# Interleaving the two matmul runs of a fused transformer block's main loop on TensorE

## What is computed

```python
nx = _layer_norm(x, ln_gamma, ln_beta)
scores = einsum('bth,bph->btp', nx @ Wq, prototype_bank @ Wk) * H ** (-0.5)
evidence = einsum('btp,bph->bth', softmax(scores), prototype_bank @ Wv)
combined = concatenate([nx, evidence, anchor], axis=-1)          # (8, 512, 768)
router_probs = softmax(combined @ router_W + router_b)
h = silu(einsum('btc,ecr->bter', combined, e_w1) + e_b1)         # 3 experts x 512
expert_out = einsum('bter,erh->bteh', h, e_w2) + e_b2
routed = sum(expert_out * router_probs[..., None], axis=-2)
g = sigmoid(silu(combined @ gate_w1 + gate_b1) @ gate_w2 + gate_b2)
out = x + g * (routed @ out_w + out_b)
```

## Time and profile before

| what | value |
|---|---|
| median of 3 runs | 465.12 us (464.63 to 465.8) |
| span of the profiled execution | 462.2 us |
| PE (TensorE matmul) busy | 451.3 us, 98% of the span |
| PEld (weight load) busy | 400.3 us, 87% |
| DVE, ACT, POOL busy | 263.2, 236.0, 143.4 us |

### The profile page before, as it was taken

The page is one execution under the profiler, slowest core; times in us unless marked ns, Lnnn a source line. Parts: engine busy times, 40 slices in busy tenths (PEclk is TensorE's granted clock), DMA queues, the critical chain, the costliest instruction groups (busy, mean ns, idle before and its releaser), DMA issues.

```text
span 462.2 us, 7383 instructions
## 1 busy us (share of the span) xinstructions
PE 451.3 (98%) x2771; PEld 400.3 (87%) x2771; DVE 263.2 (57%) x574; ACT 236.0 (51%) x361; POOL 143.4 (31%) x200
## 2 busy tenths in 40 slices
PE   4999999999999999999999999999999999999995
PEld 4588888898988899898988999898988998988895
DVE  3567366758566554648456554648456655425336
ACT  1337455675645456634755456544754555644341
POOL 4104701009505620293005520392006520282000
PEclk9999999999999999999999999999999999999998
DMA  8577406121221322222311322222310312221001
GB/s 239 194 214 265 138 2 139 22 45 25 88 60 36 68 93 46 47 48 68 92 23 24 68 92 48 45 48 70 91 37 10 70 46 48 45 47 47 0 1 45
DMA packets 24611, 32.78 MB, mean 71 GB/s; under 512 B 1864, under 2 KB 16000, under 8 KB 24576
## 3 DMA queue, kind: packets, MB, share of 16 engines
q1 hardware_dynamic: 24256, 31.76, 26.4%
q0 software_dynamic: 240, 0.53, 0.5%
q10 hardware_dynamic: 80, 0.02, 0.0%
HBM read 13.40 MB, written 4.19 MB: 38 GB/s over the span
## 4 chain that ended last, share of the span: by engine, by line
PE 96%; DMA 1%; DVE 1%; issue 0%; SPq 0%; ACT 0%
PE bank L418 37%; PE bank L674 34%; PE bank L650 11%; PE bank L516 2%; PE bank L446 2%; PE bank L429 2%; PE bank L559 2%; PE bank L483 1%; DMA work<-in_ctx_dram 1%; PE bank L528 1%; PE bank L448 1%; PE bank L587 1%; PE bank L469 1%; PE bank L504 1%; PE bank L540 1%; PE bank L459 1%
## 5 line engine op out<-in xcount | busy, mean ns | idle before, releaser
L418 PE MATMUL bank<-nx,w1n 128*128 128x512 f32 x672 | 175.7, 397 | 0.0
L1106 DVE TENSOR_TENSOR h<-hf,h 128x512 fp32r<-128x512 f32 x112 | 83.5, 745 | 160.2 <-ACT h L828 159.3
L674 PEld LDWEIGHTS bank<-w,h 128*128 128x128 f32 x1152 | 149.8, 190 | 8.2
L674 PE MATMUL bank<-w,h 128*128 128x256 f32 x1152 | 152.0, 282 | 0.0
L825 ACT ACTIVATE hf<-bank,zb 128x512 f32<-128x512 f32 x112 | 77.2, 689 | 144.1 <-PE bank L650 143.9
L418 PEld LDWEIGHTS bank<-nx,w1n 128*128 128x128 f32 x672 | 119.3, 188 | 19.8
L828 ACT ACTIVATE h<-bank,zb 128x512 fp32r<-128x512 f32 x112 | 76.2, 681 | 0.0
L650 PE MATMUL bank<-wT,vw 128*128 128x512 f32 x224 | 69.9, 393 | 0.0
L1140 POOL TENSOR_TENSOR rstd<-ve,minus_half 128x4 f32<-128x4 f32 x8 | 9.1, 1136 | 159.1 <-DVE ve L853 159.1
L650 PEld LDWEIGHTS bank<-wT,vw 128*128 128x128 f32 x224 | 41.9, 188 | 9.0
L1150 POOL TENSOR_SCALAR work<-b2o,ph 128x256 f32<-128x256 f32 x32 | 20.8, 649 | 78.3 <-DVE ph L933 76.0
(11 more groups left out here) (127 smaller groups left out, 407.0 us busy)
## 6 DMA issues: line engine op xcount, KB each, us to landing
vw<-vw_pair SPq DMA_DIRECT2D x48, 256.0 KB, 3.7
stage<-in_L_xcond_e_w_dram SPq DMA_DIRECT2D x9, 512.0 KB, 4.5
xbuf<-in_x_dram SPq DMA_DIRECT2D x8, 512.0 KB, 4.4
out_dram<-xbuf SPq DMA_DIRECT2D x16, 256.0 KB, 2.1
vw<-vw_pair SPq DMA_DIRECT2D x16, 130.0 KB, 2.6
w1v<-in_L_xcond_e_w_dram SPq DMA_DIRECT2D x3, 512.0 KB, 6.3
work<-in_ctx_dram SPq DMA_DIRECT2D x1, 512.0 KB, 6.0
stage<-in_L_xcond_gate_w_dram SPq DMA_DIRECT2D x2, 256.0 KB, 9.6
```

The costliest lines, as they stand in the source:

```text
L418: mm = pe.matmul(dst, lhs(a), rhs(c), start=first and i == 0, stop=last and i == n - 1)
L674: mm = pe.matmul(o, h[:, s % HRING, a, t * PART:(t + 1) * PART], rhs, start=c == 0 and i == 0 and t % 2 == 0, stop=c == COUNT[g] - 1 and i ...
L1106: dve.tensor_tensor(h[:, s % HRING, LO, :], hf[:, s % 2, :], h[:, s % HRING, HI, :].bitcast(F32), ALU.subtract).then_inc(s_hlo, 1)
```

## The change

TensorE's two runs of a slot are issued in turn: one 512-wide matmul of block s, one 256-wide matmul of block s - 2, eight times, and then the four 256-wide ones that are left. The helpers `first_layer_nx`, `first_layer_evidence` and `second_layer` become `first_layer(s, i)` and `second_layer(s, n)`, which issue one matmul each; each wait is at the matmul that it stood at before. Slots 0 and 1, which have no second layer, keep their order, and so do the last two turns, which have no first layer. No instruction is added or taken away, and no other engine's order changes.

```diff
-            def first_layer_nx(s):
+            NX_PASSES = KC * len(SPLIT_PASSES)
+            Z_PASSES = NX_PASSES + 2
+            W_PASSES = NT * len(SPLIT_PASSES)
+
+            def first_layer(s, i):
...
+                dst = bank[ZB[s % 3]][:, :]
+                if i < NX_PASSES:
+                    k, (a, c) = i // len(SPLIT_PASSES), SPLIT_PASSES[i % len(SPLIT_PASSES)]
+                    pe.matmul(dst, w1n[:, a, k, j * PART:(j + 1) * PART], nx[:, b % 2, c, k, :],
+                              start=i == 0, stop=False)
+                    return
...
+                part = i - NX_PASSES
+                mm = pe.matmul(dst, vw[:, part, RP + j * PART:RP + (j + 1) * PART],
+                               wT[:, b % 2, :], start=False, stop=part == LO)
+                if part == LO:
+                    mm.then_inc(s_z, 1)
...
+            def second_layer(s, n):
...
+                t, i = divmod(n, len(SPLIT_PASSES))
+                half = t // 2
+                u = 2 * (NG * b + g) + half
+                if n == 0:
+                    pe.wait_ge(s_hlo, s + 1)
...
+                if c == 0 and t % 2 == 0 and i == 0:
+                    take(AB[u % 3], (s_comb, u + 1))
...
             for s in range(SLOTS + LAG):
                 b, j = divmod(s, NB)
+                if s == 0:
+                    for i in range(NX_PASSES, Z_PASSES):
+                        first_layer(s, i)
                 if s < SLOTS:
-                    if s == 0:
-                        first_layer_evidence(s)
                     run_plan(steps, "pe", b, j, "pre")
-                    if s >= EARLY:
-                        first_layer_nx(s)
-                    if s > 0:
-                        first_layer_evidence(s)
+                if 0 < s < LAG:
+                    for i in range(NX_PASSES, Z_PASSES):
+                        first_layer(s, i)
                 if s >= LAG:
-                    second_layer(s - LAG)
+                    for i in range(W_PASSES):
+                        if i < Z_PASSES and s < SLOTS:
+                            first_layer(s, i)
+                        second_layer(s - LAG, i)
```

More of the change, by code:

```diff
@@ L657, in second_layer @@
                 c = j - FIRST[g]
[L658 to L665, removed]
-                    u = 2 * (NG * b + g) + half
-                    if c == 0:
-                        take(AB[u % 3], (s_comb, u + 1))
-                    for t in (2 * half, 2 * half + 1):
-                        o = bank[AB[u % 3]][:, (t % 2) * H:(t % 2 + 1) * H]
-                        for i, (a, w) in enumerate(SPLIT_PASSES):
-                            rhs = gw2[:, w, c, :] if g == 0 else w2[:, w, j - GB, :]
-                            mm = pe.matmul(o, h[:, s % HRING, a, t * PART:(t + 1) * PART], rhs,
-                                           start=c == 0 and i == 0 and t % 2 == 0,
-                                           stop=c == COUNT[g] - 1 and i == 2 and t % 2 == 1,
-                                           skip_group_check=True)
-                    if half == 0 and c == COUNT[g] - 1:
-                        mm.then_inc(s_acc, 1)
@@ new lines, in second_layer @@
+                if c == 0 and t % 2 == 0 and i == 0:
+                    take(AB[u % 3], (s_comb, u + 1))
+                a, w = SPLIT_PASSES[i]
+                rhs = gw2[:, w, c, :] if g == 0 else w2[:, w, j - GB, :]
+                last = t % 2 == 1 and i == len(SPLIT_PASSES) - 1
+                mm = pe.matmul(bank[AB[u % 3]][:, (t % 2) * H:(t % 2 + 1) * H],
+                               h[:, s % HRING, a, t * PART:(t + 1) * PART], rhs,
+                               start=c == 0 and i == 0 and t % 2 == 0, stop=c == COUNT[g] - 1 and last,
+                               skip_group_check=True)
@@ L681, in second_layer @@
+                if last and c == COUNT[g] - 1:
                     mm.then_inc(s_acc, 1)
-                else:
+                elif last and half == 1:
                     mm.then_inc(s_w2, 1)
-            first_layer_nx(0)
+            for i in range(NX_PASSES):
+                first_layer(0, i)
             b2_product()
             w_transpose(0)
-            first_layer_nx(1)
+            for i in range(NX_PASSES):
+                first_layer(1, i)
             logits(0)
```

22 lines of the change are left out of this document (20 added, 2 removed).

## The result

The changed kernel takes 472.5 us (median of four runs, 471.69 to 473.09), the kernel before 465.09 in the same comparison (464.63 to 465.8): 7.4 us more, a ratio of 1.0156 with a 95% interval from 1.0139 to 1.0172. The prediction was 470.5 us, slower, in a range of 463.0 to 475.5.

What follows compares the result with a forecast made beforehand. PE's matmuls were taken to bound the kernel. Waits and end +8.0 us, cheaper pairs -3.1, longer waits from a shorter PE path +0.5: +5.4 on 465.12 gives 470.5 us, range 463.0 to 475.5.

Steps and rivals of the forecast that it cites:

- PE sets the time, and a matmul costs its distance to the next start: Whole kernel: PE busy 451.3 of 462.2 us, so time is the sum of matmul costs plus waits the new order makes.
- A pair at 344 ns, -3.1 us: Interleaved slots: one 512-wide plus one 256-wide costs 344 ns instead of 348, over 770 new pairs; between -6.2 and +2.3 us.
- 1.06 us of slack used up at every boundary: Group boundaries: matmul 6 asks for `combine` of half 0 1.06 us earlier; fourteen of 31 boundaries wait, 5.9 us.
- the rule: Group boundaries: each wait of matmul 6 is 1.06 us plus 0.05 for the semaphore, less the boundary's slack before.
- The price of a wait, 0.05 us on top: Group boundaries: each of the fourteen waits costs about 0.05 us more for the semaphore.
- Slack above zero is free: Group boundaries: seventeen with slack of 1.17 us or more, above the 1.06 us shift, stay free of waits.
- Slot 2 and slot 12: First batch: matmul 0 waits for L1106 in slot 2, +0.65 us; `w_transpose` waits behind DVE in slot 12, +0.6 us.
- Nothing else waits in the loop: Main loop: matmul 0 in later slots asks 2.44 us earlier against a smallest slack of 2.6, so stays free.
- The end, +0.83: Block 111: DVE's last chain hangs on the last first-layer matmul, which comes seven 256-wide matmuls later, +0.83 us.
- Rival 1: Pairs: a matmul's extra cost goes when widths alternate, pair 330 ns, 461.2 us; decides from 335 ns; chance 0.16.
- Rival 2: Group boundaries: the ACT and DVE chain gets shorter, so the 5.9 us of waits don't come, 464.1 us; chance 0.12.
- Rival 3: Pairs: each switch of bank and moving tile costs 5 ns, 10 a pair, 479.8 us; chance 0.10.

Runs made afterwards that it cites:

- A2: Changed kernel with DVE's `combine` of half 0 moved ahead of L1106, PE's order untouched: 465.17 us, ratio 1.0004 to the kernel before.
- B4: Kernel before, not interleaved, plus a DVE instruction of about 1 us ahead of `combine` of half 0 at group boundaries: 472.06 us, ratio 1.0138.
- A4: Changed kernel, but the two runs kept apart in the 32 slots whose second layer is a group's first block: 466.58 us, ratio 1.0029.
- B1: Changed kernel with A2's DVE order and the two runs kept apart in the first batch and slot 111: 462.22 us against 465.41, ratio 0.9935.
- B2: B1 with two 512-wide and three 256-wide matmuls in turn, four times a slot, instead of one and one: 467.21 us, ratio 1.0036.
- C1: Changed kernel with matmul 6's wait for `combine` moved onto the 512-wide matmul before it: 477.58 us against 465.4, ratio 1.0266.
- B3: Kernel before, but the 256-wide matmuls in the middle blocks of each expert alternate between their two banks: 465.35 us, ratio 0.9998.
- A1: Changed kernel, but slot 111, the last with a first layer, keeps its two runs apart: 471.44 us, ratio 1.0144.

## Why the prediction was right, and where it was short

- **PE sets the time, and a matmul costs its distance to the next start.** Right; with it the account closes to 0.1 us. The granted clock isn't full in every slice, as the prediction has it: the last slice of the earlier trace rows reads 8. It falls behind PE's last matmul, so nothing hangs on it.
- **A pair at 344 ns, -3.1 us.** The mean came out there (-3.3 us over some 770 new pairs, 4.3 each), but not for the reason given. I took a value between the costs at a switch and those inside a run. In fact more than half of the pairs have the lower bound of 340, and in 25 of the slots the mean is 348 to 349, near the upper one. All eleven slots that begin with 512-wide products are of the dear kind, but so are fourteen others; what decides is open, and the value of 344 is luck as much as reasoning. The Trainium skill ("TensorE: Matmul & The Clock Gate", "Back-to-back issue gap") has a formula for the gap of an isolated warm matmul, by which a pair would be estimated at 109 + 216 = 325 ns; the cheapest pairs here have 340, so taking the rows was right.
- **1.06 us of slack used up at every boundary.** Right, and the heart of the case: fourteen waits were predicted and fourteen came, at the very boundaries named, 6.0 us against 6.4. A2 removed them by DVE's order alone, B4 made thirteen of them by delay alone. That the sum came out so near is partly luck. In slots 16 and 18 the rule gives 1.06 and 0.49 us and the trace 0.53 and 0.02: in slot 16 PE had already lost 0.5 on the same path, at the pair product below, and in slot 17 L1106 took 1.24 us before and 0.73 in the changed kernel, for a reason that no run shows. The other twelve came to 5.4 us where the rule gives 4.7 with the cheaper pairs. The chain through ACT and DVE wasn't "as long as before" there: at nine of them it was 0.04 to 0.10 us longer, 0.7 in all.
- **The price of a wait, 0.05 us on top.** This is the step that fell short. A wait ends 0.05 to 0.06 us behind its releaser, as assumed, but then costs the restart of 0.105 as well: 14 x 0.105 = 1.5 us. It could have been read from the kernel before. In the earlier trace rows the first boundary has a slack of 0.05, and there two 256-wide matmuls have a duration of 0.51, where at the second boundary, with more slack, three have 0.52: one matmul's cost, 0.11, was lost already. The 0.05 there was no slack but the semaphore's own time; matmul 6 waited. I used the row for the slack and didn't look at what the small slack cost.
- **Slack above zero is free.** Also wrong, for 0.6 us. Matmul 6 in slot 32 of the changed kernel, PE:

```profile
173.38 0.40 PE L654 MATMUL bank<-wT,vw 128*128 128x512 f32 x1
173.62 0.35 PE L680 MATMUL bank<-w,h 128*128 128x256 f32 x1
173.81 0.40 PE L654 MATMUL bank<-wT,vw 128*128 128x512 f32 x1
```

It isn't late (0.24 behind its neighbour) and still takes 0.19 instead of 0.115. Its load could run ahead by a part only. The traces give the size: where half 0 was read 0.05 us ahead of matmul 6, matmul 6 took 0.105 us more; with 0.075 it took 0.09 more, with 0.09 it took 0.07, with 0.115 (B4) 0.04, and with 0.16 or more (A4, A2) nothing. Read time and extra cost add up to 0.16 us throughout, the semaphore's 0.055 and a load's 0.105. So to be free a matmul needs what it waits for 0.16 us ahead here, not just in time. The six boundaries hit are those that had 1.17 us before, which the prediction counted as free; another near miss is matmul 0 of slot 15.

- **Slot 2 and slot 12.** +0.65 and +0.6 against 0.8 and 0.7. The like of slot 12 in slot 4, up to 0.4 us, I had missed, though `fold_lo` stands there too. Slot 12, DVE and then PE:

```profile
92.32 1.29 DVE L955 TENSOR_TENSOR w<-bank,w 128x512 fp32r<-128x512 f32 x2
```

```profile
93.76 0.43 PE L459 MATMUL bank<-ident_r,wcat 128*128 128x128 f32 x3 [0.70 <-DVE w L955]
```

- **Nothing else waits in the loop.** Wrong once, in slot 16, by 0.5 us. I read the slacks of matmul 0 and matmul 6, not those of the steps that PE takes between. One of the first batch's pair products (L418) was nearly late before:

```profile
109.05 0.36 PE L418 MATMUL bank<-work_hi 128*128 128x260 f32 x1 [0.35 <-issue]
```

The profile names no releaser for it, but the program and the timeline do. The product takes bank 7, which the transposes of slot 15 filled and DVE's L877 (L868 before) reads last; it starts 0.10 us behind the end of L877 here (109.05 and 108.95) and in A2 (108.35 and 108.25), and 0.40 behind it before (106.09 and 105.69). L877 moved by 3.26 us from one trace to the other and PE's matmuls ahead of the product by 2.45, so the product lost 0.8 us of its lead. That these 0.8 are the 0.83 by which a slot's first layer ends later fits in size, but isn't shown; B1, which leaves the first batch apart, doesn't have the wait.

- **The end, +0.83.** Right: 0.84 in the trace, and from the last 512-wide matmul to the end it is as long as before, as predicted. DVE at the end:

```profile
462.83 0.69 DVE L1115 TENSOR_TENSOR h<-hf,h 128x512 fp32r<-128x512 f32 x1 [0.65 <-DVE work L1094]
...
465.49 0.69 DVE L1104 TENSOR_TENSOR work<-bank,work 128x512 f32<-128x512 f32 x1
```

From L1106 of block 111 to L1095 it is 2.66 us in both (454.20 to 456.86 in the earlier trace rows, 462.83 to 465.49 here, under the new line numbers).

- **The rivals.** Rival 1 needed a pair of under 335 ns; it is 340 to 350. Rival 2, no waits because the chain gets shorter, was wrong for the change, but A4 shows that the chain can get shorter when other slots move (3.21 for 3.53 to 3.55). Rival 3 is out for one and one; B2 shows that some mixed orders do cost more.

Together: the predicted 5.4 us, plus the restarts 1.5, near misses 0.6, slot 16 0.5 and small differences at slot 2 and slot 12, less 0.4 and 0.2 for boundary waits and pairs that came out lower, is 7.7 us in the trace and 7.4 in the medians.

## What to carry to other kernels

When two runs of instructions are interleaved on the engine that bounds a kernel, count how far each wait moves against the work that releases it, and compare that with the slack at every hand-over; here 1.06 us of shift against slacks of 0.05 to 0.99 decided the result, while the gain that was there (4 ns a pair) is visible only when the consumer's order is moved with it. Price a new wait on a matmul as its length plus a restart, and count slack as free only if it covers the semaphore and the weight load too, 0.16 us here. The repair is often on the other engine: putting the read that PE needs ahead of one that nobody hurries for gave back 7.3 us.

## What the hardware showed

- **The restart.** A matmul that has waited for a semaphore takes 0.10 to 0.115 us more, at 256 wide and at 512 wide, in alternating and in plain order (14 of 14 waits in the changed kernel, and in B4, C1, A4). In the trace its weight load starts with it instead of ahead of it. A matmul whose releaser ended less than 0.16 us ahead pays a part of it (0.04 to 0.09 us). 0.106 us is also the pace of the nearly empty matmuls.
- **Pairs of one and one cost 341 to 345 ns** as the mean of a slot in 85 slots and 348 to 349 in 25, against 348 in separate runs; two and three make the second 512-wide matmul mostly cost 235 to 241. I have no mechanism for it, and no run here settles it.
- **The output bank of neighbouring 256-wide matmuls has no price** (B3: 409.40 against 409.44 us of loop).
- **A stretch at half clock.** In three of the twelve traces (the changed kernel, A1, B3) the granted clock is 0.50, that is 1.2 GHz, between about 36 and 39 us, behind a stretch in which PE was busy without a gap. PE was just as busy there in the trace of before, where the clock stayed full, so what brings the stretch on is open. In B3 it costs 1.6 us (from block 1's last first-layer matmul to slot 3, 9.27 against 7.65 us in the kernel before), in the changed kernel 0.5, because there it covers waits of slots 2 and 4. It comes with either order, so it isn't the change's doing, and it is a reason to cut a trace behind the start before two kernels are compared.
